# Vision tower with a mixture of experts: bias products in row groups, the slot inversion in column halves by pieces, and the last spectrum group by units

## What is computed

```python
logits = t @ gate_w.T + gate_b                    # 1088 tokens of 192, 8 experts
top_val, top_idx = jax.lax.top_k(logits, 2)
score = jax.nn.softmax(top_val, axis=-1)
cw = zeros((T, E)).at[arange(T)[:, None], top_idx].add(score)
for e in range(E):
    he = gelu(t @ w1[e].T + b1[e])
    ye = he @ w2[e].T + b2[e]
    out = out + cw[:, e:e + 1] * ye
return x + out
```

## Time and profile before

| | |
|---|---|
| median of three runs | 814.05 us |
| the profiled execution's own time | 816.31 us |
| its span, first to last instruction | 814.4 us |
| TensorE busy | 86% of the span |
| VectorE, ScalarE, GpSimd busy | 66%, 54%, 53% |
| mean granted TensorE clock | 0.927 |

### The profile page before, as it was taken

One profiled execution on the slowest core, in us unless ns is written; L12 is line 12 of the kernel. 1 busy time (PEld: TensorE's weight loads), 2 busy tenths in 40 slices (PEclk: granted clock), 3 DMA queues, 4 the chain that ended last, 5 costly groups with the idle time before them and its releaser, 6 DMA issues. The chain is left out here.

```text
span 814.4 us, 22164 instructions
## 1 busy us (share of the span) xinstructions
PE 699.3 (86%) x8537; PEld 595.3 (73%) x8537; DVE 533.5 (66%) x1058; ACT 440.0 (54%) x864; POOL 428.7 (53%) x375
## 2 busy tenths in 40 slices
PE   4999999999999225788888888998899889999980
PEld 4788888888888124688787888677467677999970
DVE  3899999999999312465555555697668773555544
ACT  1788888888888512354444454232453221766640
POOL 4666677767676243777777776000200202567751
PEclk9999999999999657889999999999899965999995
DMA  9874569865996296565554554200000684233424
GB/s 244 202 194 143 149 180 259 231 186 139 266 268 269 49 228 181 152 169 155 152 145 141 147 150 136 81 2 1 1 2 2 254 252 149 37 58 58 58 29 126
DMA packets 78519, 114.90 MB, mean 141 GB/s; under 512 B 8791, under 2 KB 58108, under 8 KB 78076
## 3 DMA queue, kind: packets, MB, share of 16 engines
q1 hardware_dynamic: 61246, 76.80, 33.5%
q0 software_dynamic: 14336, 35.40, 16.8%
q10 hardware_dynamic: 2880, 1.90, 0.7%
HBM read 91.83 MB, written 22.25 MB: 140 GB/s over the span
## 5 line engine op out<-in xcount | busy, mean ns | idle before, releaser
L598 PE MATMUL psum<-power,tT 128*128 128x192 f32 x864 | 162.4, 345 | 65.4 <-DVE tT L725 65.1
L598 PEld LDWEIGHTS psum<-power,tT 128*128 128x128 f32 x864 | 148.1, 200 | 76.3 <-DVE tT L725 41.4
L539 POOL DMA_INDIRECT rows<-power_table,rank_row x144 | 146.4, 1017 | 65.9 <-issue 54.0
L725 DVE SCALAR_TENSOR_TENSOR tT<-rows,swaps,scaled 128x384 f32<-128x384 f32 x144 | 82.8, 616 | 120.7 <-ACT scaled L653 120.1
L331 PE MATMUL ps<-dft,fold 112*64 112x97 f32 (+1 forms) x3072 | 147.2, 249 | 11.6 <-POOL fold L295 11.6
L653 ACT ACTIVATE scaled<-rows,swaps 128x384 f32<-128x384 f32 x144 | 80.3, 606 | 138.8 <-DMA rows<-power_table,rank_row 135.5
L331 PEld LDWEIGHTS ps<-dft,fold 112*64 112x64 f32 (+1 forms) x3072 | 141.9, 131 | 16.6 <-issue 11.9
L302 POOL TENSOR_TENSOR ss<-uv 97x388 f32<-97x388 f32 x96 | 82.3, 880 | 76.7 <-ACT uv L373 76.7
L405 DVE TENSOR_TENSOR folded<-ps,far 112x388 f32<-112x388 f32 x192 | 98.5, 554 | 25.6 <-ACT far L361 25.5
L295 POOL TENSOR_TENSOR fold<-img 112x896 f32<-112x896 f32 x48 | 103.6, 2160 | 14.5 <-DMA img<-in_x 9.9
L422 DVE TENSOR_TENSOR uv<-ps,odd 97x388 f32<-97x388 f32 x192 | 97.8, 551 | 2.0 <-ACT odd L366 2.0
(11 more groups left out here) (174 smaller groups left out, 938.6 us busy)
## 6 DMA issues: line engine op xcount, KB each, us to landing
img<-in_x SPq DMA_DIRECT2D x48, 784.0 KB, 5.0
power_table<-power SPq DMA_DIRECT2D x16, 576.0 KB
power<-in_w_tok SPq DMA_DIRECT2D x3, 1728.0 KB, 10.3
power<-in_w SPq DMA_DIRECT2D x8, 579.0 KB, 7.3
power<-in_w SPq DMA_DIRECT2D x4, 1152.0 KB, 11.0
rows<-power_table,rank_row POOLq DMA_INDIRECT x144, 3.1
power_table<-power SPq DMA_DIRECT2D x1, 1200.0 KB
power_table<-power SPq DMA_DIRECT2D x1, 1072.0 KB, 15.4
```

Source lines behind the costliest of these rows:

```text
L539: pool.indirect_dma_start(out=rows[:, j % RING, half, :], out_offset=None, in_=table[0:RECORDS if j % CHUNKS < PLAIN else RECORDS + P * (L ...
L598: last = pe.matmul(ps[:, q % 2, 0:DIM], points[:, j % SWAPPED, c, s].rearrange("p h b -> p (h b)"), wt[:, c, s, chunk, :], start=(chunk == ...
L725: last = dve.scalar_tensor_tensor(out=points[:, j % SWAPPED].rearrange("p c s h b -> p (c s) h b")[:, :, half, :], in0=kept, scalar=swaps[ ...
```

## The change

1. **Bias products.** `cw` becomes [128, 12, 32] with zeros beyond the 8 experts (one memset, before the last `top_two`). Three transposes of four tiles each (128 x 128) replace nine, one ScalarE copy (128 x 384) replaces three. `b2` is stored four times, from partition 0, 32, 64 and 96 on (a [128, 192] constant, 96 KB to load where there were 6 KB). The nine products take their eight rows from partition 32 (t mod 4) on, each of the four row positions with a PSUM bank of its own, and signal once.
2. **Slot inversion.** `at_lane` is made in three pieces of six n, after the token marks. The share marks move from VectorE to GpSimd, which waits for `share` and `at_tile`. TensorE waits per piece, and each product is split into a product for lanes 0 to 63 and one for lanes 64 to 127, in different column halves of the array.
3. **Additions.** VectorE adds the biases of the first three tiles before `found`, the other six after `target`, ahead of the weight copies.
4. **Spectrum's end.** For the last group GpSimd sums each unit's squares when they are there, and ScalarE roots each unit when it is summed.

```diff
+        def sum_unit(u):
+            g, i0 = u // UPG, u % UPG * 2
+            pool.wait_ge(sq_done, u + 1)
+            for s in range(2):
+                last = pool.tensor_tensor(ss[:, g % SS_RING, s, i0:i0 + 2], uv[:, g % UV_RING, s, i0:i0 + 2, 0:FREQ],
+                                          uv[:, g % UV_RING, 1 - s, i0:i0 + 2, FREQ:PAIR], ALU.add)
+            last.then_inc(ss_done, 1)
...
+            if isinstance(t, int) and t == GROUPS + SUM_LAG - 1:
+                pool.wait_ge(root_done, GROUPS - SS_RING)
+                for u in range(UNITS - UPG, UNITS):
+                    sum_unit(u)
+            elif not isinstance(t, int) or t >= SUM_LAG:
...
+        def root_units(g):
+            act.wait_ge(root_room, g + 1)
+            for n in range(UPG):
+                act.wait_ge(ss_done, UPG * g + n + 1)
+                image = g % PASS_GROUPS * G_IMGS + n * 2
+                last = act.activation(R[:, g // PASS_GROUPS % R_BUFS, :, :, image:image + 2].rearrange("p k s i -> p s i k"),
+                                      ss[:, g % SS_RING, :, n * 2:n * 2 + 2], ACT.Sqrt)
+            last.then_inc(root_done, 1)
...
-    BIAS_BANK = (6, 7, 0, 5, 4)
+    BIAS_BANK = (6, 7, 0, 5)
+    PIECES = 3
+    PIECE = TOPK * TT // PIECES
+    def bias_at(t):
+        bank = BIAS_BANK[t % ROW_GROUPS] if t // ROW_GROUPS < 2 else 4
+        at = t // ROW_GROUPS % 2 * DIM
+        return psum[:, bank, at:at + DIM]
...
     def program_pool(pool):
+        pool.wait_ge(share_set, 1)
+        pool.wait_ge(ah, 4)
+        for k in range(TOPK):
+            last = pool.tensor_tensor(sent_of[:, k, :, 1, :], tiles_at[:, k],
+                                      share[:, :, k, None].to_broadcast([P, TT, MT]), ALU.mult)
+        last.then_inc(shares_marked, 1)
...
-        pe.wait_ge(cw_set, 1)
+        pe.wait_ge(cw_set, 2)
+        for n in range(SETS):
+            last = pe.transpose(psum[:, 3, n * P:(n + 1) * P],
+                                cw[:, n * ROW_GROUPS:(n + 1) * ROW_GROUPS, :].rearrange("p t e -> p (t e)"), W["identity"])
+        last.then_inc(cw_tr, 1)
+        pe.wait_ge(cwT_done, 1)
         for t in range(TT):
+            rows = slice(t % ROW_GROUPS * GROUP, t % ROW_GROUPS * GROUP + EXPERTS)
+            last = pe.matmul(bias_at(t), cwT[rows, t // ROW_GROUPS, :], W["b2"][rows, :], start=True, stop=True)
+        last.then_inc(b2_mm, 1)
+        for piece in range(PIECES):
+            pe.wait_ge(marked, 2 + piece)
+            if piece == 0:
+                pe.wait_ge(shares_marked, 1)
+            for n in range(piece * PIECE, (piece + 1) * PIECE):
+                for half in ROW_HALVES:
+                    last = pe.matmul(psum[half, 2, 0:2 * MT], at_lane[:, n, half], sent[:, n].rearrange("p a m -> p (a m)"),
+                                     start=(n == 0), stop=(n == TOPK * TT - 1))
         last.then_inc(found, 1)
...
+        act.activation(cwT[:, :, :].rearrange("p n t -> p (n t)"), psum[:, 3, 0:SETS * P], ACT.Copy).then_inc(cwT_done, 1)
...
+            if n == NC - 1:
+                dve.memset(cw[:, :, :], 0.0).then_inc(cw_set, 1)
             top_two(n)
...
+        for piece in range(PIECES):
+            part = slice(piece * PIECE, (piece + 1) * PIECE)
+            dve.tensor_tensor(at_lane[:, part, :], W["lanes"][:, None, :].to_broadcast([P, PIECE, P]),
+                              at_f[:, 0, part, None].to_broadcast([P, PIECE, P]), ALU.is_equal).then_inc(marked, 1)
...
+        dve.wait_ge(b2_mm, 1)
+        for t in range(NC):
+            add_bias(t)
         dve.wait_ge(found, 1)
...
+        for t in range(NC, TT):
+            add_bias(t)
         dve.wait_ge(slot_done, 2)
```

More of the change, by code:

```diff
@@ L393, in step @@
                 square(t - SQ, j - SQ)
-            if (j - RT) % UPG == 0 and (dyn or t >= RT):
+            if not dyn and t == UNITS - UPG + RT:
+                root_units(GROUPS - 1)
+            elif (j - RT) % UPG == 0 and (dyn or t >= RT):
                 root((t - RT) // UPG, (j - RT) // UPG)
@@ L1283, in experts @@
     pick = sb("pick", [P, TOPK, TT, EXPERTS])
-    cw = sb("cw", [P, TT, EXPERTS])
-    cwT = sb("cwT", [EXPERTS, TPAD])
+    ROW_GROUPS = 4
+    GROUP = P // ROW_GROUPS
+    SETS = -(-TT // ROW_GROUPS)
+    cw = sb("cw", [P, SETS * ROW_GROUPS, GROUP])
+    cwT = sb("cwT", [P, SETS, P])
     both = sb("both", [P, TT + 1, EXPERTS])
@@ L1492, in program_scalar @@
         act.wait_ge(cw_tr, 1)
-        for b in range(3):
-            n = min(4, TT - 4 * b) * P
-            act.activation(cwT[:, b * 4 * P:b * 4 * P + n], psum[0:EXPERTS, 3 + b, 0:n], ACT.Copy).then_inc(cwT_done, 1)
+        act.activation(cwT[:, :, :].rearrange("p n t -> p (n t)"), psum[:, 3, 0:SETS * P], ACT.Copy).then_inc(cwT_done, 1)
         act.activation(e21[:, 0:1], e21[:, 0:1], ACT.Gelu)
@@ L1579, in program_vector @@
         dve.wait_ge(share_set, 1 + TOPK)
-        dve.tensor_tensor(cw[:, :, :], shared[:, 0], shared[:, 1], ALU.add).then_inc(cw_set, 1)
+        dve.wait_ge(cw_set, 1)
+        dve.tensor_tensor(cw[:, 0:TT, 0:EXPERTS], shared[:, 0], shared[:, 1], ALU.add).then_inc(cw_set, 1)
         dve.wait_ge(route_mm, 1)
@@ L1634, in program_vector, with add_bias @@
         last.then_inc(marked, 1)
-        for k in range(TOPK):
-            last = dve.tensor_tensor(sent_of[:, k, :, 1, :], tiles_at[:, k],
-                                     share[:, :, k, None].to_broadcast([P, TT, MT]), ALU.mult)
-        last.then_inc(marked, 1)
+        for piece in range(PIECES):
+            part = slice(piece * PIECE, (piece + 1) * PIECE)
+            dve.tensor_tensor(at_lane[:, part, :], W["lanes"][:, None, :].to_broadcast([P, PIECE, P]),
+                              at_f[:, 0, part, None].to_broadcast([P, PIECE, P]), ALU.is_equal).then_inc(marked, 1)
         dve.tensor_copy(tile_expert[:, :], tile_f[:, :]).then_inc(slot_done, 1)
         c.end()
-        for t in range(TT):
-            dve.wait_ge(b2_mm, min(TT, t // 2 * 2 + 2))
-            dve.tensor_tensor(x_all[:, t, :], psum[:, BIAS_BANK[t // 2], t % 2 * DIM:(t % 2 + 1) * DIM], x_all[:, t, :],
-                              ALU.add).then_inc(biased, 1)
+        def add_bias(t):
+            dve.tensor_tensor(x_all[:, t, :], bias_at(t), x_all[:, t, :], ALU.add).then_inc(biased, 1)
+        dve.wait_ge(b2_mm, 1)
+        for t in range(NC):
+            add_bias(t)
         dve.wait_ge(found, 1)
```

23 lines of the change are left out of this document (5 added, 18 removed).

## The result

The changed kernel took 805.34 us in the median of four runs (803.77 to 808.02), the kernel before beside it 814.28 (811.93 to 817.74): a ratio of 0.9889, 95% interval 0.9851 to 0.9927, or 9 us less. The forecast was 808.8 with a range from 805.8. The profiled execution has a span of 802.1 us and took 804.04 (before: 814.4 and 816.31), at a mean granted clock of 0.937 (before: 0.927).

What follows compares the result with a forecast made beforehand. Routing was taken as bound nearly all the way by TensorE, with VectorE's marks almost as late. Terms -5.4 + 0.2 - 0.2 + 0.1 = -5.3 us, from a median of 814.05, gave 808.8; range 805.8 to 812.1.

Steps and rivals of the forecast that it cites:

- the first tile, taken "as before": Head of the tile loop: the first tile was to run as before, with no term in the sum.
- The inversion and its marks, -5.4: Routing: marks in pieces and paired column halves at 109 ns end the inversion at 676.35 instead of 681.78, -5.4 us.
- The rival without a collision: Routing marks: VectorE and GpSimd don't collide on the port, pieces begin at 671.25; -6.2 in all, 807.9; chance 0.14.
- the one with GpSimd shut out: Routing marks: GpSimd waits until VectorE's pieces are through, inversion ends at 678.1; -3.6 in all, 810.4; chance 0.12.
- the one of the rising clock: Inversion: the clock rises in it and the marks set its end; -6.9 in all, 807.1; chance 0.08.
- halves don't pay: Inversion: half products don't overlap, a pair takes 194 or 218 ns; 811.8 or 812.6, the no-gain cases; chance 0.09.
- The size of the collision: Routing marks: VectorE and GpSimd take turns on the shared SBUF port, so VectorE's pieces come 0.9 us later.
- The memset, costed at nothing: Routing: the `cw` memset fits VectorE's wait for the last logits and costs nothing; if in the way, about 0.4 us.
- Behind `found`, +0.2: After the inversion: later `x_all` stores cross the first fetches, weight copies no longer do; +0.2 us, bounds -0.2 and +0.9.
- the slower rival: Head of the tile loop: the clock rises later; 10.6 us more low time eats the gain, 17 gives 817.3; chance 0.03.
- The spectrum's end, -0.2: Last spectrum group: ScalarE's 0.38 us idling goes, a second half root costs 0.1 to 0.2; -0.2, bounds -0.4 and +0.2.
- The larger constant, +0.1: Start: SP's issue of the larger constant takes 0.43 instead of 0.34 us; +0.1, bounds 0 and +0.5.

Runs made afterwards that it cites:

- x5: Changed kernel with the share marks back on VectorE instead of GpSimd; ratio 0.9910 to the kernel before.
- x6: Changed kernel with 36 full-width inversion products instead of column halves, same three pieces; ratio 0.9988 to the kernel before.
- x19: Changed kernel with all additions before `found`, share marks on VectorE, four dummies instead of two, constants loaded behind the image loads; 804.85 us, ratio 0.9882 to the kernel before.
- x8: Changed kernel with all nine bias additions ahead of `found`, none behind it; ratio 0.9939 to the kernel before.
- x13: Changed kernel with all additions before `found`, share marks on VectorE, four dummies instead of two, constants loaded behind the image loads; ratio 0.9894 to the kernel before.
- x9: Changed kernel with four dummy products instead of two behind the inversion; ratio 0.9900 to the kernel before.
- x2: Kernel before with only the new spectrum's end (last group summed and rooted by units); 812.68 us, ratio 0.9967 to the kernel before.
- x3: Changed kernel without the new spectrum's end, so the routing edits alone; 809.06 us, ratio 0.9947 to the kernel before.
- x11: Kernel before with only the constant `b2` enlarged to 96 KB, its first eight rows used; ratio 0.9985 to the kernel before.
- x15: Kernel before with only the new bias products; marks, full-width inversion and additions as before; ratio 0.9945 to the kernel before.

## Why the prediction was right and where it was wrong

The direction and the mechanism in routing were right, and the stages that the change touches gave -4.4 us where -5.3 were forecast. Two steps failed: the first tile, taken "as before", cost 1.0 us, and the range left too little room for the spread of single executions, which is why the measured 805.34 lies below it. In the first two profiles the rest of the difference, 7.6 of 12.3 us, is in stages whose instructions are the same in both kernels, and by the later comparisons the first four executions of the changed kernel were unusually fast ones.

**The inversion and its marks, -5.4: right.** From the last logits to `source` the profile has -5.49. Step by step: `cw` ends at 657.45, transposes 0.55 (forecast 0.5), the copy 0.49 (0.51), the products 1.38 (2.3 at most; they ran in a stretch at nearly full clock, which I had not foreseen, and which is worth nothing, since the marks come later; in x5, x6 and x19 they ran at 0.50 and took 2.28). The inversion begins 6.87 us after `cw` (forecast 6.9) and takes 4.10 (3.9 and a drain of 0.25). GpSimd's two operations take 1.34 (1.0). One reading was wrong without harm: the clock was not at 1.2 GHz "throughout" in the kernel before, whose nine transposes ran at 1.00 (window 665.40 to 666.50); the earlier trace rows begin behind them. The rival without a collision, the one with GpSimd shut out, and the one of the rising clock fall by the rows above; x6 against the changed kernel rules out that halves don't pay. The rule of the Trainium skill against the halves (TensorE: Matmul & The Clock Gate, section "Part 3: Packing small matmuls — row/col tiling") does not hold here. With loads that wait for the matmuls a pair would have taken the 194 ns or more that the prediction worked out from its rows; 36 pairs took 4.08 us, 113 ns each, with both loads in the same rows. With the port rule of the Trainium skill (SBUF — State Buffer, section "SBUF: two separate sides") the traces agree: 1.04 against 0.68, 3.04 against 2.69 with GpSimd's marks taken away. The size of the collision was near too: 0.9 forecast, 0.36 and 0.35, together 0.7, measured.

**The memset, costed at nothing: right.** In the changed kernel it takes 0.38 us and ends before the last logits, and `cw` begins 4.90 us after these in both kernels. But from the last logits to `at_tile` it is 8.96 to 9.04, mostly 9.04, in the kernels with the padded `cw`, and 8.90 or 8.91 in all five profiles without it. The 0.13 lies in one place, between the two operations that make `at_i` and the copy to `at_f` (0.34 us from start to start, 0.20 before), whose instructions are the same in both; why is not shown.

**Behind `found`, +0.2: mis-sized.** It is +0.65 (4.48 to between 5.05 and 5.18), inside the bounds of -0.2 and 0.9. The step that failed is the choice between them: I let the freed weight copies count against the stores. Nearly all of it is in the first fetch, from its issue to its landing: 2.94 us before, 3.54 in the changed kernel. With all additions first it is 3.18 in x8 and 3.3 in x13, which would make the stores' share up to 0.4, but 3.54 again in x19 with the same order. So how much of it is the stores', and what the rest is, isn't shown.

**The first tile, taken as "as before": wrong, +1.0.** This is the mechanism of the slower rival, a longer low stretch at the head of the tile loop, at a price that I had not put in the sum: 6.5 to 6.8 us of low clock instead of 3.4, in nine of the ten profiles with two dummies and the new routing (not in x5's). I had given it a chance of 0.03 because I asked for 10.6 us of it, enough to eat the gain; at a third of that size it came nearly every time, and the prediction's own sign, low clock that lasts longer behind the fetch, came true. The argument "the same dummies and the same wait stand there before and after" was wrong in both halves. The dummies are the same instructions, but they take 2.7 to 3.3 us where they took 3.4 to 3.8, since the clock rises 1.4 to 2.5 us after `source` where it rose 2.6 to 3.7 after; and the rows come 0.6 later. So TensorE is idle for 1.5 to 2.0 us instead of 0.5 to 0.9. What the first tile lost was then shown to be in the dummies' hands: 8.00 us with four (x9).

**The spectrum's end, -0.2: mis-sized, -0.6** (x2 and x3). Two half roots take 1.49 us together where the whole one took 1.51; the fixed part of 0.1 to 0.2 for the second isn't there. The idling of 0.38 is gone, and the halves start 0.2 us before the recorded end of the root ahead of them, as roots and squarings elsewhere in a filled queue do.

**The larger constant, +0.1: as forecast** by its issue (0.44 us in x11), and nothing that could be told from none in the time.

**The sum and the range.** The terms come to -5.49 + 0.65 + 1.04 - 0.60 = -4.4 us, against -5.3: 0.9 apart. The first result, -9, is lower, and the step that failed there is the range: its lower end, 805.8, was the 807.1 of the high-clock case less 1.3 us for "a run's spread", taken from three runs that lay 2.6 us apart. The spread of single executions is 2 to 4 us (standard deviation) for nearly every kernel here, from stages that no edit touches: 6 us lie between the forms of attention, 6 between the ends of the spectrum. No term of the sum failed by the 3.5 us between 808.8 and 805.34; the largest error, the first tile's, points the other way. As far as the later executions tell, the first four were a lucky draw: two of them, 803.77 and 804.04, lie below 805.8, and of the 32 later ones of the same kernel one does (803.84). All 36 have a median of 810.6 us and the 81 of the kernel before beside them 814.4, 4.0 apart in the means. (The upper end, 812.1, was called the better of the two no-gain cases; that was 811.8.) Over four comparisons the changed kernel gave 0.9889, 0.9978, 0.9933 and 0.9939, 0.9935 in the mean, or -5.3 us; weighted by their intervals 0.9953, or -3.9. The -4.4 of the stages and the -5.3 of the forecast both lie in that neighbourhood, and nothing here tells the one from the other. The four differ by more than their own intervals allow (0.9978 and 0.9889 exclude each other), so a comparison has more uncertainty than its interval says. What it is that changes between comparisons is open; the chip is one thing that did, and no run tried it by itself. Open too is what decides whether attention gets its low stretches: no experiment here moved them.

## What to carry to other kernels

Split a chain of products whose stationary operand is wide and whose moving one is narrow (here 128 against 48 float32 columns) into column halves: the pace was that of the weight load, and two halves of the columns ran at once. When such a cut empties TensorE just ahead of a wait, look at what the clock does behind it, and size the dummies to end when the data lands, by their length at the clock that they will run at. Check a difference of a few us by the stages of several profiles, and put what lies in untouched stages into the range, not into the change; and an engine that helps with two SBUF inputs beside VectorE may cost as much as it carries.

## What the runs showed of the hardware that I had not expected

- The same instructions of one stage took between 131.8 and 138.1 us, in step with 1.9 to 16.2 us of low clock in it.
- The four matmuls of the same two dummies took between 2.71 and 3.75 us, by where in them the clock rose, and the idle time behind them went with 0, 3.4 or 6.8 us of low clock.
- Eighteen bias matmuls in four row groups took 2.28 us at a granted clock of 0.50 (x5, x6, x19) and 1.24 at 1.00 (x15); the same products in one row group took 6.10 at 0.50.
- Two roots of 388 columns took no longer than one of 776: 1.49 and 1.51 us.
- SP's single issues at the start take 0.3 to 0.5 us, some of them 1.0 to 3.0, and the image load behind them moves by it; where the constants stand behind the image loads the last root ended within 0.13 us in three profiles.
